# A gated delta rule recurrence: the states turned by the product that updates them

## The reference

```
Sk = einsum('bhvk,bhk->bhv', S, k_t)
S  = a_t[..., None] * S - (b_t[..., None] * (Sk - v_t))[..., None] * k_t[:, :, None, :]
o_t = einsum('bhvk,bhk->bhv', S, q_t)
```

## Time and profile before

| | |
|---|---|
| median of 3 runs | 2928.49 us (2927.63 to 2932.69) |
| the profiled execution | 2931.77 us, span 2930.0 us |
| granted TensorE clock, mean | 0.878 of 2.4 GHz |
| TensorE matmul busy | 77% of the span |
| VectorE busy | 66% |
| ScalarE busy | 45% |

### The profile page before, as it was taken

One profiled execution on the slowest core, in us unless ns is written; L12 is line 12 of the kernel. 1 busy time (PEld: TensorE's weight loads), 2 busy tenths in 40 slices (PEclk: granted clock), 3 DMA queues, 4 the chain that ended last, 5 costly groups with the idle time before them and its releaser, 6 DMA issues.

```text
span 2930.0 us, 67669 instructions
## 1 busy us (share of the span) xinstructions
PE 2243.2 (77%) x24976; PEld 1691.7 (58%) x24976; DVE 1919.4 (66%) x4412; ACT 1319.4 (45%) x2752; POOL 559.3 (19%) x546
## 2 busy tenths in 40 slices
PE   5999888888863777677777777777776776399998
PEld 3455666666653666666666666666666665234443
DVE  4223777777773777777777777777777777523334
ACT  2002666666661534454454445445444543044434
POOL 0000333333333212212221221122122212200000
PEclk9999999999986978988897888889789878599999
DMA  5001444555555333333333333343333333301110
GB/s 216 7 13 38 192 188 193 200 200 206 207 207 190 114 104 131 125 110 106 130 115 106 131 122 116 99 135 112 111 128 121 114 100 117 140 33 72 72 57 22
DMA packets 139483, 358.77 MB, mean 122 GB/s; under 512 B 11312, under 2 KB 92968, under 8 KB 126424
## 3 DMA queue, kind: packets, MB, share of 16 engines
q1 hardware_dynamic: 139176, 354.92, 34.1%
q0 software_dynamic: 48, 0.16, 0.0%
HBM read 226.97 MB, written 128.07 MB: 121 GB/s over the span
## 4 chain that ended last, share of the span: by engine, by line
PE 48%; issue 20%; ACT 12%; DVE 11%; POOL 6%; DMA 3%; DVEq 0%; SPq 0%; POOLq 0%; ACTq 0%
PE PS L1306 9%; ACT arena L680 5%; PE PS L1412 4%; PE PS L1439 4%; PE PS L1294 3%; PE PS L1345 3%; ACT arena L685 3%; PE PS L1169 3%; PE PS L1217 3%; PE PS L1320 3%; POOL arena L487 2%; PE PS L1333 2%; DMA arena<-beta_d 2%; PE PS L1265 2%; PE PS L1233 2%
## 5 line engine op out<-in xcount | busy, mean ns | idle before, releaser
L1192 PE MATMUL PS<-arena 128*128 x2048 | 491.0, 399 | 98.8 <-DVE arena L886 97.9
L886 DVE SCALAR_TENSOR_TENSOR arena<-PS,SM,arena 128x256 f32<-128x256 f32 x1152 | 468.6, 476 | 124.9 <-ACT arena L596 122.2
L1192 PEld LDWEIGHTS PS<-arena 128*128 128x128 f32 x2048 | 395.8, 195 | 194.0 <-DVE arena L886 114.0
L1306 PE MATMUL PS<-arena 128*128 128x128 f32 x1920 | 312.0, 311 | 113.1 <-ACT arena L685 109.5
L1306 PEld LDWEIGHTS PS<-arena 128*128 128x128 f32 x1920 | 262.4, 212 | 156.7 <-ACT arena L685 151.3
L525 POOL TENSOR_TENSOR arena<-arena 128x256 f32<-128x256 f32 x128 | 98.6, 770 | 1265.4 <-DVE arena L985 1265.4
L680 ACT ACTIVATE arena<-arena 128x128 f32<-128x128 f32 x960 | 302.1, 395 | 0.0
L929 DVE TENSOR_TENSOR arena<-arena,PS 128x512 f32<-128x512 f32 x192 | 127.5, 685 | 246.7 <-PE PS L1345 246.6
L596 ACT ACTIVATE arena<-PS,SM 128x256 f32<-128x256 f32 x384 | 207.6, 565 | 152.3 <-PE PS L1192 148.7
L660 ACT COPY arena<-PS 128x512 f32<-128x512 f32 x154 | 90.2, 586 | 411.5 <-PE PS L1233 195.5
L1294 PE MATMUL PS<-ident,arena 128*128 128x128 f32 x960 | 171.2, 307 | 31.0 <-ACT arena L680 30.7
(11 more groups left out here) (138 smaller groups left out, 3871.6 us busy)
## 6 DMA issues: line engine op xcount, KB each, us to landing
arena<-g_d SPq DMA_DIRECT2D x128, 512.0 KB, 4.2
vas_d<-arena SPq DMA_DIRECT2D x24, 2048.0 KB, 6.9
arena<-vas_d SPq DMA_DIRECT2D x128, 384.0 KB, 3.4
kq_d<-arena SPq DMA_DIRECT2D x8, 4096.0 KB, 11.4
arena<-kq_d SPq DMA_DIRECT2D x16, 2048.0 KB, 9.4
arena<-beta_d SPq DMA_DIRECT2D x8, 2048.0 KB, 8.1
kb_d<-arena SPq DMA_DIRECT2D x8, 2048.0 KB, 13.9
arena<-kb_d SPq DMA_DIRECT2D x16, 1024.0 KB, 6.4
```

What stands on the lines that cost most here:

```text
L886: nc.vector.scalar_tensor_tensor(acc, raw[:, :, i:i + PT_], CW[:, w, i, hh:hh + 1], acc, ALU.mult, ALU.add).then_inc(job_free if i == TAPS ...
L1192: ins = mm(dst.rearrange("p (b n) -> p b n", b=B), W4[:, w, kt, DH * h:DH * (h + 1)], XNT[:, kt, :, bass.ds(c * PT_ + (HALO - halo), halo ...
L1306: ins = mm(bank(7)[:, 128 * gi:128 * (gi + 1)].rearrange("v (l x) -> v l x", l=NB), STR[:, s % 2, gi, :], KQ[d][:, :, p0:p0 + 2].rearrange ...
```

## The change

The new update adds everything in the accumulator of TensorE, and turns the state while it does so. A matmul gives the transposed left operand times the right one. In even chunks S comes in with values on rows; TensorE multiplies S with a diagonal matrix of the decays (DIAG, made by ScalarE from the identity, in the place of STR), which gives the decayed state with keys on rows, and adds KBT times PT32. ScalarE copies the sum to S (`state_out`), and the reads take S itself, without transposes or STR. For this PT32 must hold decayed rows: VectorE multiplies P32 with the decay at the start of block 0, TensorE transposes it again at the start of block 1 (`late_transposes`, 16 of them) and ScalarE copies it (`late_copy`, four). In odd chunks S comes in with keys on rows; TensorE multiplies it with the identity, which turns it, and adds PT32 times KBT; ScalarE scales out of PSUM into S (`decay`), and transposes, copies to STR and reads follow as before. Keys are negated when they are evacuated to KBT, so the sum needs no subtraction, and `state_add` is gone.

The slots are laid out anew: `STEP_AT` gives one update with its two slots to each of blocks 1, 2, 3, 5, 6 and 7, and two to block 4. In odd chunks the first update is made ahead of its step and update u + 1 stands in step u, between the transposes and the reads of the second slot. In the even chunks reads use banks 6 and 7 in turn. GpSimd clears P32 too at the start.

```diff
+STEP_AT = [[], [0], [1], [2], [3, 4], [5], [6], [7]]
...
+        DIAG = STR
...
+            for tile in (S, PT32, KBT, P32):
...
+                if what == "kt":
+                    nc.scalar.mul(dst, src, -1.0).then_inc(pa_done, 1)
...
+                def diagonals(s):
                     j, g0 = slot_pairs(s)
-                    act.wait_ge(s_updated, n * 16 + s + 1)
+                    if s == 0:
+                        act.wait_ge(e_in[c], i * 16 + 16)
+                    elif s >= 2:
+                        act.wait_ge(up_psum, n * 8 + s // 2)
                     for gi in range(4):
                         p = 4 * (g0 + gi) + j
-                        ins = nc.scalar.mul(S[:, p, :], S[:, p, :], EX[c][:, 6, p:p + 1])
+                        ins = nc.scalar.mul(DIAG[:, s % 2, gi, :], ident[:, :], EX[c][:, 6, p:p + 1])
+                    ins.then_inc(diag_ready, 1)
+                def state_out(s):
+                    j, g0 = slot_pairs(s)
+                    act.wait_ge(up_psum, n * 8 + s // 2 + 1)
+                    nc.scalar.copy(S.rearrange("v (g j) k -> v j g k", j=4)[:, j, g0:g0 + 4],
+                                   bank(4 + s % 2).rearrange("v (g k) -> v g k", g=4)).then_inc(s_scaled, 1)
+                def decay(s):
+                    j, g0 = slot_pairs(s)
+                    act.wait_ge(up_psum, n * 8 + s // 2 + 1)
+                    for gi in range(4):
+                        p = 4 * (g0 + gi) + j
+                        ins = nc.scalar.mul(S[:, p, :], bank(4 + s % 2)[:, 128 * gi:128 * (gi + 1)], EX[c][:, 6, p:p + 1])
                     ins.then_inc(s_scaled, 1)
+                def late_copy(q):
+                    act.wait_ge(late_psum, i * 4 + q + 1)
+                    nc.scalar.copy(PT32[:, 4 * q:4 * q + 4].rearrange("r g v -> r (g v)"), bank(4 + q)).then_inc(late_ready, 1)
...
+                    if m == 1 and nxt and not c:
+                        for q in range(4):
+                            late_copy(q)
+                    if m == 1 and nxt and c:
                         act.wait_ge(e_in[c], i * 16 + 16)
-                    if reads:
-                        decay(reads[0])
+                        decay(0)
                     if keys:
                         act.wait_ge(corr_full, n * 9 + 2 + m)
                         if m == 3:
                             act.wait_ge(kb_in[d], (i + c) * 16 + 16)
                         key_copy(c if m == 1 else d, *keys)
-                    for k, s in enumerate(reads):
-                        if k == 0 and len(reads) > 1:
-                            decay(reads[1])
-                        state_copy(s)
-                        if k < 2:
+                    if m == 0 and nxt and not c:
+                        diagonals(0)
+                        diagonals(1)
+                    if m == 1 and nxt and c:
+                        decay(1)
+                    for u in steps:
+                        a, b = 2 * u, 2 * u + 1
+                        later = u == steps[-1]
+                        if c:
+                            state_copy(a)
                             next_evac()
-                        if 0 < k < len(reads) - 1:
-                            decay(reads[k + 1])
-                        read_copy(s)
+                            read_copy(a)
+                            state_copy(b)
+                            if u < 7:
+                                decay(a + 2)
+                            next_evac()
+                            read_copy(b)
+                            if u < 7 and not later:
+                                decay(b + 2)
+                        else:
+                            state_out(a)
+                            state_out(b)
+                            next_evac()
+                            read_copy(a)
+                            next_evac()
+                            read_copy(b)
+                            if u < 7:
+                                diagonals(a + 2)
+                                if not later:
+                                    diagonals(b + 2)
                     while evacs:
                         next_evac()
                     if m < NB - 1 or nxt:
                         corr_copy(m)
+                    if steps and steps[-1] < 7:
+                        if c:
+                            decay(2 * steps[-1] + 3)
+                        else:
+                            diagonals(2 * steps[-1] + 3)
...
+                        if nxt and not c:
+                            dve.wait_ge(pt_psum, 1 + n * N_PT)
+                            dve.wait_ge(e_in[c], i * 16 + 16)
+                            tt(P32, P32, EX[c][:, 6].unsqueeze(2).to_broadcast([128, NP, 32]), ALU.mult).then_inc(p32_late, 1)
...
+                def late_transposes():
+                    P = P32.rearrange("v p t -> v (p t)")
+                    pe.wait_ge(p32_late, i + 1)
+                    pe.wait_ge(corr_sub, n * N_SUB + 16)
+                    for g in range(16):
+                        ins = nc.tensor.transpose(bank(4 + g // 4)[:, 128 * (g % 4):128 * (g % 4 + 1)], P[:, 128 * g:128 * (g + 1)], ident[:, :])
+                        if g % 4 == 3:
+                            ins.then_inc(late_psum, 1)
...
                 def update(u):
                     if u == 0:
                         pe.wait_ge(corr_sub, n * N_SUB + 16)
                     else:
-                        pe.wait_ge(s_updated, n * 16 + 2 * u)
+                        pe.wait_ge(s_scaled, n * 16 + 2 * u)
+                    if not c:
+                        pe.wait_ge(late_ready, i * 4 + max(2, u // 2 + 1))
+                        pe.wait_ge(diag_ready, i * 16 + 2 * u + 2)
+                    for gi in range(4):
+                        for b in range(2):
+                            j, g0 = slot_pairs(2 * u + b)
+                            mm(bank(4 + b)[:, 128 * gi:128 * (gi + 1)], S[:, 4 * (g0 + gi) + j, :], ident[:, :] if c else DIAG[:, b, gi, :], start=(gi == 0), stop=False)
                     for gi in range(4):
                         for b in range(2):
                             j, g0 = slot_pairs(2 * u + b)
                             rows = slice(32 * j, 32 * j + 32)
-                            ins = mm(bank(4 + b)[:, 128 * gi:128 * (gi + 1)], PT32[rows, g0 + gi, :], KBT[rows, g0 + gi, :], start=True, stop=True)
+                            left, right = (PT32, KBT) if c else (KBT, PT32)
+                            ins = mm(bank(4 + b)[:, 128 * gi:128 * (gi + 1)], left[rows, g0 + gi, :], right[rows, g0 + gi, :], start=False, stop=(gi == 3))
                     ins.then_inc(up_psum, 1)
...
+                    else:
+                        pe.wait_ge(s_scaled, n * 16 + s + 1)
+                        if s < 2:
+                            pe.wait_ge(late_ready, i * 4 + 3 + s)
+                        else:
+                            pe.wait_ge(x_read, n * 16 + s - 1)
...
                     if m == 1 and nxt:
-                        update(1)
+                        if c:
+                            update(0)
+                        else:
+                            late_transposes()
+                    for u in steps:
+                        a, b = 2 * u, 2 * u + 1
+                        if c:
+                            state_transposes(a)
+                            next_prep()
+                            reads_of(a)
+                            state_transposes(b)
+                            if u < 7:
+                                update(u + 1)
+                            next_prep()
+                            reads_of(b)
+                        else:
+                            update(u)
+                            next_prep()
+                            reads_of(a)
+                            next_prep()
+                            reads_of(b)
```

86 lines of the change are left out of this document (33 added, 53 removed).

## The result

The changed kernel took 3094.11 us (median of 4 runs, 3088.34 to 3108.24) against 2929.05 us before (4 runs, 2927.63 to 2932.69): a ratio of 1.057, with an interval of 1.053 to 1.061. The forecast was 3045 us, range 2975 to 3110. So the sign and the mechanism hold, and the loss is 165 us where 116 were forecast.

A forecast was written before the change was run, and what follows sets the result against it. TensorE's queue, with ScalarE's copies between its groups, was taken as the bound, not VectorE. 8 x 2.8 + 7 x 13.2 + 1.7 = 116.5 us on 2931.8 gave 3048, at the median 3045 us; range 2975 to 3110.

The forecast's parts named there:

- What bounds the kernel: Blocks 2 and 4: TensorE's queue with ScalarE's copies between its groups sets them; VectorE's state additions lie mostly in idle time.
- The product at 2.0 us an update: Each update: the eight added full 128x128 matmuls on TensorE take 2.0 us, with bounds of 0.88 and 4.1.
- Odd chunks, +13.2: Seven of the 15 chunks: block times sum to 115.8 us, 13.2 us longer each.
- kt ahead of the copies: Odd chunks, block 5: ScalarE's evacuation of kt stands ahead of read_copy(10) and state_copy(11), which come only after it, at 9.25.
- Even chunks, +2.8: Eight of the 15 chunks: block times sum to 105.4 us, 2.8 us longer each.
- Rival 2: Blocks 1 to 4: TensorE stays at 2.4 GHz, so 37 us of added clock loss go: 3008 us; chance 0.18.
- Rival 3: Blocks 1 and 2: the low clock level lasts as it does now, 15 x 4.8 us more: 3117 us; chance 0.12.
- Rival 1: Whole recurrence: VectorE is the bound and the additions come off the path whole, 136 us less: 2794 us; chance 0.08.
- Rival 4: Both chunk kinds: queues overlap so well that the waits put on ScalarE vanish, 121 us: 2924, no change; chance 0.07.
- VectorE's busy time down by 136 us: Profile after: VectorE loses 240 additions, 154 us, and gets eight multiplications, 18 us, so busy time falls by some 136 us.
- The memset, +1.7: Ahead of the first chunk: clearing P32 too adds 1.7 us, 2048 of 12288 elements of 10.41 us.
- P32's multiplication in the head's shadow: Chunk's head: VectorE's eight multiplications of 2.28 us fall where it waits for carried products anyway; 18 us without that cover.

The follow-up runs named there:

- run 1: Changed kernel with the state's product with identity or diagonals left out of each update: 2893.0 us, ratio to before 0.987.
- run 2: Kernel before with eight full 128x128 matmuls of state and identity put ahead of each update: 2988.1 us, ratio 1.019.
- run 3: Kernel before without VectorE's 240 subtractions of the update from the state, decay waiting for the update itself: 2883.0 us, ratio 0.984.
- run 6: Changed kernel with TensorE's and ScalarE's queues of odd chunks in another order: 3068.3 us, ratio to before 1.048.
- Run 7: Changed kernel with unread matmuls added in TensorE's two idle stretches in block 4 of even chunks: 3073.8 us, ratio to before 1.049.
- run 4: Changed kernel with a third slot of diagonals, so the even slot's are made during the update before: 2989.7 us, ratio to before 1.020.
- run 9: Changed kernel with the first step's reads moved ahead of the first sel item in block 4: 2986.0 us, ratio to before 1.019.

## Why the prediction was right, and where its sizes were off

*What bounds the kernel.* Right: runs 1, 2 and 3 priced the three parts. VectorE's 153 us were worth 48, TensorE's product cost 201 in the new queue and 57 in the old one.

*The product at 2.0 us an update.* Right in odd chunks (1.96). In even chunks it was 2.76, for the clock.

*Odd chunks, +13.2.* Measured +14.7. Every block came within 0.6 us but for 5 and 6 (1.3 and 1.2 more), where the clock was at 0.82 and 0.81 and not at the upper level that the sum took. The order of ScalarE's queue (kt ahead of the copies) was right: run 6.

*Even chunks, +2.8.* This is the term that was mis-sized: +8.7. The waits were the ones named, at the places named. What was too small is what the clock adds to them. The sum had 1.5 us in block 1, where the level stayed at 0.99, and 1.0 in block 4; measured were 4.5 us more than forecast in block 4 and 1.4 and 1.5 in blocks 2 and 3, which I had at the upper level. Run 7 shows that 4.9 us of block 4 go when the two waits are filled with work, and that half of it comes back in other blocks, so for the whole chunk it shows 2.6 us to be the clock's; run 4 shows that blocks 2 and 3 are at 9.7 and 11.0 us when neither wait nor low level is there. One even chunk of eight, the fifth, did have a block 4 of 23.7 us, the forecast, with the low stretch in block 3 instead (15.2). 8 x 5.9 + 7 x 1.5 = 58 us is nearly the whole miss of the profiled execution, 3108 for 3048; at the median it is 49. That the range held 3094 is in part luck: its upper end was drawn for an update of up to 2.6 us at one level, and not for low stretches behind new waits.

*Rival 2 (the clock stays up).* The rule of the Trainium skill (TensorE: Matmul & The Clock Gate, "Part 4: PE-mode transpose"), that the full clock doesn't engage for transposes, is not tested by any run: run 2, where full matmuls in the old queue brought the clock to 1.00 in every block but 0 in 12 of 15 chunks, added them without taking transposes away. It doesn't decide here in any case: the changed queue has as many of them and the clock fell to 0.64. In the seventh chunk, after block 0, each low stretch began behind or within one in which TensorE stood idle for 1.7 to 3 us. I had the rival as a gain; it should have been read from the other side, as what a new wait costs beyond its own length.

*Rival 3 (the low level lasts in blocks 1 and 2)* came nearer in size (3117) than the forecast, at another place: its blocks 1 and 2 have 0.99 and 0.87 in the even chunk. *Rival 1* fell by run 3. *Rival 4* fell by runs 4 and 6: the waits on ScalarE were there and could be taken away.

*VectorE's busy time down by 136 us.* It was 81. The extensions of P (L941, now L990) got slower, 109 of them with 112.9 us of busy time for 74.2, which is 39 of the missing 55 us. One of 256 columns takes 0.42 us ahead of block 1 of the first chunk, where GpSimd does nothing, and two take 2.11 us in the sixth, where they run beside GpSimd's output operation:

```profile
939.08 0.42 DVE L990 TENSOR_TENSOR arena<-arena 128x256 f32<-128x256 f32 x1
...
1532.58 1.20 POOL L527 TENSOR_TENSOR arena<-arena 128x256 f32<-128x256 f32 x1
...
1533.09 2.11 DVE L990 TENSOR_TENSOR arena<-arena 128x256 f32<-128x256 f32 x2
```

Over the whole trace the 16 of this size with no GpSimd operation beside them take 0.42 us each, and the 47 with one 0.94 to 0.97; in the kernel before, where in several blocks the subtractions (L935) stand between the chain and these, the 47 took 0.56 to 0.95. That GpSimd is the cause was not tried by itself. In the block shown VectorE stands idle for 1.65 us behind them until the corrections come, so there they cost nothing.

*The memset, +1.7:* 12.16 for 10.41 us. Right. *P32's multiplication in the head's shadow:* nearly. It stands ahead of the first L975, so by this cut it lies in block 7 of the odd chunk, 11.1 us for 10.5; block 0 of the even chunks is shorter, 13.0 for 13.9. In the first chunk it is in the open: VectorE's first addition (L1013) starts at 930.1 us where L964 started at 927.0, a cost of 3 us that the sum didn't have.

Left open: why an even chunk sometimes has its low stretch in block 3 and not in 4, which may be what moves one execution against another (3088 to 3108); and what in block 1 of odd chunks brings the clock down between its fifth and ninth us. The trace shows a wait just ahead of it, TensorE's for decay(0), which run 6 left in place:

```profile
1513.40 0.66 PE L1374 MATMUL PS<-ident,arena 128*128 128x128 f32 x4 [1.24 <-ACT arena L702]
```

## What to carry to other kernels

Price a change of queue by laying the new order of each engine side by side, block by block: it gave the places of the waits that mattered here, and in runs 4, 6 and 9 small edits took waits away. Then look for what each new wait does to TensorE's clock: here the groups behind a stretch of 2 to 3 us of idling took nearly double, and taking away 8.4 us of waits (by the prices) gave 14.7 us in an even chunk. And before trading one engine's work for another's, move what stands in a queue ahead of a late wait: two lines changed in the old kernel were worth 50 us and 65 to 99, as much as the whole change gave in the best form tried.

## What the runs showed of the hardware

The granted clock rose with added work: in run 2, 128 more full matmul instructions a chunk brought blocks 1 to 4 from 0.57, 0.76, 1.00 and 0.81 to 1.00 each and cost 57 us for 240 us of added TensorE time. It fell while TensorE stood idle for 2.96 and 2.80 us, and was 0.50 for 6.8 us behind the first and for over 14 us behind the second, though TensorE was busy for 11.2 of these 14.4 us; it was 1.00 again in blocks 5 and 6 of odd chunks when a wait of 1.44 us went (run 6). VectorE's extension of 256 columns took 0.42 us alone and 0.94 to 0.97 beside a GpSimd operation.
